# Three semaphore rises of TensorE an expert in place of eight, in the expert stage of a one-core transformer layer

## The reference

```python
x = layernorm(x + attention(x))     # 16 heads of 64, causal, one null key
x = layernorm(x + ffn(x))
# ffn: 4096 tokens, E = 32 experts, 4 of them a token, cap = 640 rows an expert
w, idx = gate(xf, wg)                               # top 4 of 32
xe = xp[buf_tok].reshape(E, cap, 128)               # rows gathered for each expert
h = silu(xe @ w1[e]) * (xe @ w3[e])
out = (h @ w2[e]) * buf_w                           # each row by its gate weight
y = zeros.at[buf_tok].add(out)                      # back to the tokens
z = silu(xf @ sw1) * (xf @ sw3) @ sw2               # shared expert, all tokens
return y + z
```

## Time and profile before

| | |
|---|---|
| device time, median of 3 runs | 905.85 us (905.0 to 906.47) |
| profiled execution, first to last instruction | 977.5 us |
| TensorE busy in it | 859.0 us (88%) |
| VectorE, ScalarE, GpSimd busy | 654.3, 616.8, 673.5 us |

### The profile page before, as it was taken

One profiled execution on the slowest core, in us unless ns is written; L12 is line 12 of the kernel. 1 busy time (PEld: TensorE's weight loads), 2 busy tenths in 40 slices (PEclk: granted clock), 3 DMA queues, 4 the chain that ended last, 5 costly groups with the idle time before them and its releaser, 6 DMA issues. The chain is left out here.

```text
span 977.5 us, 25690 instructions
## 1 busy us (share of the span) xinstructions
PE 859.0 (88%) x9439; PEld 633.9 (65%) x9439; DVE 654.3 (67%) x2448; ACT 616.8 (63%) x1189; POOL 673.5 (69%) x580
## 2 busy tenths in 40 slices
PE   5789999999999999999999999766688888888654
PEld 2367777777777777777777777654465666666422
DVE  7757788987987987987987986836243434343217
ACT  3668889888888888888898787733132323233305
POOL 7656665699698699699689689346665555556636
PEclk9989999999999999999999999978798989899968
DMA  5787788645444454354354342016333323333147
GB/s 160 182 255 234 231 243 220 177 107 134 97 119 111 101 135 108 89 151 107 73 141 122 72 117 64 21 51 197 119 96 100 96 79 95 95 101 99 39 191 252
DMA packets 104428, 126.62 MB, mean 130 GB/s; under 512 B 22077, under 2 KB 65426, under 8 KB 103408
## 3 DMA queue, kind: packets, MB, share of 16 engines
q1 hardware_dynamic: 95408, 109.25, 40.8%
q0 software_dynamic: 8896, 15.74, 5.2%
HBM read 33.68 MB, written 41.58 MB: 77 GB/s over the span
## 5 line engine op out<-in xcount | busy, mean ns | idle before, releaser
L2289 POOL TENSOR_TENSOR PL<-PF,PH 128x1280 f16<-128x1280 f32 x121 | 317.8, 2626 | 107.2 <-ACT PH L1632 63.7
L1854 DVE CUSTOM_DVE_ANT_0 JUNK<-PS,M 128x256 f16<-128x256 f32 (+3 forms) x512 | 225.2, 485 | 39.5 <-PE PS L1265 35.8
L1626 ACT ACTIVATE PF<-PS 128x512 f32<-128x512 f32 (+1 forms) x384 | 192.8, 520 | 80.3 <-PE PS L1298 75.4
L2332 POOL DMA_INDIRECT y_rows<-BIG,Q x150 | 145.7, 972 | 99.3 <-ACT BIG L1551 57.4
L1632 ACT ACTIVATE PH<-PF 128x1280 f16<-128x1280 f32 x128 | 162.2, 1267 | 0.6
L2322 POOL DMA_INDIRECT xe_rows<-PAY,DEST x128 | 129.3, 1010 | 42.9 <-issue 27.7
L1291 PE MATMUL PS<-Q,K 128*128 128x512 f16 (+3 forms) x512 | 148.6, 300 | 9.2 <-DMA Q<-MROW 4.9
L1315 PE MATMUL PS<-VH,PH 128*128 128x65 f16 x1280 | 141.3, 195 | 13.0 <-DVE Y L1896 8.5
L1317 PE MATMUL PS<-VH,PL 128*128 128x65 f16 x1280 | 141.3, 194 | 1.2 <-issue 1.2
L1315 PEld LDWEIGHTS PS<-VH,PH 128*128 128x128 f16 x1280 | 119.6, 98 | 35.0 <-issue 24.5
L1316 PE MATMUL PS<-VL,PH 128*128 128x64 f16 x1280 | 141.3, 194 | 0.0
(11 more groups left out here) (252 smaller groups left out, 2027.5 us busy)
## 6 DMA issues: line engine op xcount, KB each, us to landing
K<-KH SPq DMA_DIRECT2D x128, 128.0 KB, 2.3
Q<-QH SPq DMA_DIRECT2D x128, 128.0 KB, 2.4
xe_rows<-PAY SPq DMA_DIRECT2D x20, 520.0 KB, 4.2
Q<-xe_rows SPq DMA_DIRECT2D x30, 325.0 KB
K<-KL SPq DMA_DIRECT2D x64, 128.0 KB, 2.3
Q<-QL SPq DMA_DIRECT2D x64, 128.0 KB, 2.3
y_rows<-PAY SPq DMA_DIRECT2D x16, 512.0 KB, 4.9
K<-in_L_ffn_w_dram SPq DMA_DIRECT2D x96, 64.0 KB
```

The source lines that it names most:

```text
L1626: e.activation(PF[:, n % PBUF, c0:c0 + width], PS[:, k, 0:width], ACT.Exp).then_inc(s["c_exp"], 1)
L1854: e.tensor_tensor_reduce(JUNK[:, n_ttr % 2, 0:width], PS[:, base + ab, c0:c0 + width], M0[:, 512 - width:512], 1.0, -3e38, ALU.add, ALU.ma ...
L2289: e.tensor_tensor(PL[:, n % PBUF, :], PF[:, n % PBUF, :], PH[:, n % PBUF, :], ALU.subtract).then_inc(s["c_lp"], 1)
L2332: e.indirect_dma_start(out=y4[:, :], out_offset=bass.IndirectOffsetOnAxis(ap=XE[:, x_ % 6, k, 128:129].bitcast(I32), axis=0), in_=OUT[:, x ...
```

## The change

Five edits make eight rises three. `hidden` raises `s_hid` once, after all four of its products. `product` raises `s_o` once, after all five. In the loop `dense_up` raises nothing; whoever waits for it waits for the `s_o` of the `product` that stands behind it. In iterations with a `dense_down`, `turn` raises nothing; the `dense_down` behind it raises `s_turn` for both. The waits on ScalarE and VectorE are rewritten to these counts. No instruction that computes is added, taken away or moved. SyncE's waits use the same functions.

```diff
-    def rows_done(x_, k=4):
-
-        if x_ < 0:
-            return 0
-        return 2 * x_ + (1 if k < 3 else 2)
+    def ups_done(i):
+
+        return (s_o, FIRST_DENSE + i) if i < IN_LOOP else (s_dup, i - IN_LOOP + 1)
+
+    def downs_done(i):
+
+        if i < 0:
+            return None, 0
+        return (s_turn, FIRST_DENSE + i + 3) if i < IN_LOOP else (s_ddn, i - IN_LOOP + 1)
+
+    def rows_done(x_):
+
+        return max(x_ + 1, 0)
...
-        def turn(x_):
+        def turn(x_, tell=True):
...
-            i.then_inc(s_turn, 1)
+            if tell:
+                i.then_inc(s_turn, 1)
...
-                i.then_inc(s_hid, 1)
+            i.then_inc(s_hid, 1)
...
-                i.then_inc(s_o, 1)
+            i.then_inc(s_o, 1)
...
-                e.matmul(PS[:, bank, :], weights(d, m), X1TA[:, t], start=True, stop=True).then_inc(s_dup, 1)
+                u = e.matmul(PS[:, bank, :], weights(d, m), X1TA[:, t], start=True, stop=True)
+            if i >= IN_LOOP:
+                u.then_inc(s_dup, 1)
...
-            p.then_inc(s_ddn, 1)
+            p.then_inc(s_ddn if i >= IN_LOOP else s_turn, 1)
...
-                turn(x_ + 1)
+                turn(x_ + 1, tell=x_ - 1 not in DENSE_AT)
...
-            w.wait_ge(s_hid, 2 * x_ + 1)
+            w.wait_ge(s_hid, x_ + 1)
...
-                w.wait_ge(s_o, rows_done(y_, k))
+                w.wait_ge(s_o, rows_done(y_))
...
-            w.wait_ge(s_dup, 2 * i + 1)
+            w.wait_ge(*ups_done(i))
...
-            w.wait_ge(s_hid, 2 * (x_ - 1))
+            w.wait_ge(s_hid, x_ - 1)
...
-            w.wait_ge(s_hid, 2 * x_ + 2)
+            w.wait_ge(s_hid, x_ + 1)
...
-            w.wait_ge(s_dup, 2 * i + 2)
+            w.wait_ge(*ups_done(i))
...
-            w.wait_ge(s_ddn, i - 1)
+            w.wait_ge(*downs_done(i - 2))
...
-            w.wait_ge(s_ddn, i + 1)
+            w.wait_ge(*downs_done(i))
```

## The result

The changed kernel takes 931.55 us (931.19 to 933.37, 4 runs) against 906.16 us (905.0 to 907.42, 4 runs) on the same chip: ratio 1.0289, 95% interval 1.0271 to 1.0307, so 24.6 to 27.8 us slower. The forecast was 938, with 924 to 947 as its range.

A forecast was written before the change was run, and what follows sets the result against it. TensorE was taken as the bound, at 6.75 us per dense iteration. The terms 29.7 + 0.3 + 1.0 + 1.5 = 32.5 us on the timed 905.85 gave 938.3, stated as 938, range 924 to 947.

The forecast's parts named there:

- TensorE bounds the dense iterations: In the 19 iterations with a dense piece, TensorE sets the 6.75 us period; GpSimd is next at 6.4 us an expert.
- The chain of 1.48 us: From `product`'s end through `dense_silu` and `dense_times` to the next `turn`, which would have to wait for it: 1.48 us.
- 1.65 us an iteration: At `turn`, starting at 812.57 in place of 810.92 after the dense_up edit: period 8.40 us, 18 x 1.65 = 29.7 us.
- Copies later: On ScalarE, the first copy starts 1.92 us after `product`, before 0.95; results 0.97 later, paid once: 1.0 us.
- The 0.3 us behind the loop: Iteration 25, which has no up: 6.68 us against GpSimd's 6.4 us, so 0.3 us more.
- The start, 1.5 us: At experts 0 to 2, `hidden`'s single rise makes `product` wait for `times`: between 0 and 2.4 us, taken as 1.5.
- GpSimd's backlog: Work carried out of the stage's start could partly hide the new wait, giving something like 928 us; judged absent from one row.
- turn by dense_down, nothing: In the loop, `turned` starts 1.0 to 1.3 us later but stays hidden by 0.9 us before `dense_up`: no cost.
- Rises, nothing: On TensorE, a rise takes less than 0.01 us, so taking away five an iteration gives back 0.
- long iterations: Profiled dense iterations well over 6.75 us (average 8.6 from 729.5 to 885.6); timed runs were assumed to have few.
- late word: Waiters of TensorE's rises hear late, silu up to 4.9 us; rival that each rise causes it: 901 us, chance 0.05.
- the rival: TensorE's clock falls at times with 1.65 us of waiting in 8.40: 13.5 us more, 952 us, chance 0.07.

The follow-up runs named there:

- the quiet trace: The kernel before, profiled a second time with no edit: one execution of 907.01 us, span 905.3 us.
- the run with the copies ahead: The changed kernel with ScalarE's copies put ahead of `dense_silu`: 973.67 us against 906.42 us for the kernel before, ratio 1.0736.

## Why the prediction was right, point by point

- **TensorE bounds the dense iterations: right in size, with one wait overlooked.** The forecast said that its parts follow each other with no wait. They did not: `dense_down`'s load was held by the third copy, which stood as 0.77 between `turn` and `dense_down` against 0.61 after. The row at 804.94 showed it.
- **The dense_up edit is the expensive one: shown,** by itself (929.68 us) and by its removal (917.18 us). The chain of 1.48 us came out to the hundredth (784.10 to 785.58).
- **The term that was mis-sized is 1.65 us an iteration.** It measured 8.13 - 6.75 = 1.38. The new wait stands ahead of `turn` and swallows the old one behind it, and with it 0.1 us of `dense_down`'s weight load, which now runs ahead. 18 x 1.38 = 24.8 in place of 29.7.
- **Copies later: 0.97 forecast, 0.86 measured.** The first copy starts 784.63 - 782.82 = 1.81 after `product`, before 0.95. With 24.8 that is 25.7; from `hidden(6)` to the last of GpSimd's DMAs the traces have 196.10 against 170.52, 25.6. As a cost that is paid once it holds only because `dense_up`'s wait is longer and covers it. Alone, the product edit costs 0.45 an iteration: the costs of the edits do not add.
- **The 0.3 us behind the loop did not come.** GpSimd's last seven experts run without a break in both kernels.
- **The start, 1.5 us: right in size, 1.37 measured,** with part of the path wrong. It was to come from `product` waiting for `times` at experts 0 to 2. At `product(2)` that costs 0.8; the rest comes with `hidden(4)`, which waits for the silu of expert 3. In the two traces the first dense iteration comes 34.08 us behind the first `hidden` all the same (698.90 - 664.82 and 697.66 - 663.58). The reason is that the stretch up to `turn(3)`, with waits for the rows of expert 2 and for VectorE, took 20.84 us in the one and 19.47 in the other. It varies from trace to trace, from 18.1 to 20.9 without the hidden edit and from 19.5 to 22.7 with it; what sets it is open, and that it made up for the 1.37 in this pair looks like luck.
- **The whole: 24.8 + 0.9 + 1.4 = 27.1,** for a forecast of 32.5. The timed difference is 25.4, with 24.6 to 27.8 as its interval. Most of the forecast's excess is the 1.65.
- **GpSimd's backlog: overlooked, and harmless.** The forecast took one row of the first trace as a sign that GpSimd was not behind. In the quiet trace it was: its DMAs follow each other without a break until 777 us, at the end of expert 15. But by 785 us it waits for TensorE ahead of an expert, as it still does ahead of expert 23, so the backlog is gone before the end and covers nothing of the new wait.
- **turn by dense_down, nothing: right. Rises, nothing: right,** by the intervals at most 0.5 us for the turn edit and 2.1 us for eight more rises.
- **The choice that timed runs have no long iterations: right,** and it mattered. The span of the changed kernel came out at 929.4, not at 995 to 1010: that forecast took the first execution's late word for something that each profile brings.
- **The clock did not fall** in the changed kernel, but the rival was near: 1.38 us more of waiting, in the run with the copies ahead, brought the fall.

## What to carry to other kernels

A semaphore that is raised later, to save a rise, holds back everybody who could have started on the earlier half. Follow the waiters round to the engine that sets the pace: if their chain ends in a wait of that engine within the same iteration, the whole chain is paid once an iteration, and where a rise itself shows no time, there is nothing to set against it. A wait at the start of a stage can be as real as one in its loop: look for it there before calling it covered, and measure between two points that have no wait for a transfer between them. Before adding a new wait to an iteration, look for old ones close to it, on the weight loads too, since a new wait ahead of an old one swallows it, and profile a kernel twice when its span and its timed runs differ.

## What the runs showed that was not expected

- One profiled execution of the same kernel had a span of 977.5 us, the next 905.3. In the first, waiters of TensorE's rises started up to 4.9 us later than was due; doubling the rises did not bring it back (span 902.6). What brought it is open.
- The granted clock stayed at 1.00 with 1.48 us of idle time in each 8.13 us, and fell to 0.91, by turns of the 2.4 and the 1.2 GHz level, with 2.86 us in each 9.5 to 11. The Trainium skill, "TensorE: Matmul & The Clock Gate", section "HAM oscillation — how this bites in real kernels", tells of a kernel whose matmul bursts, with a DMA wait between each two, all start at the lower clock. The second case here agrees in part, since only every other period was slow; in the first none was.
